# Six bases of layer two taken out of the TensorE contraction and added by VectorE, in a two-relation graph network on one core

## The chip, the cores and the metric

The kernel runs on one core of one Trainium2 chip. The metric is device time in microseconds of the whole launch, the median over several runs. A profiled execution gives a span (first to last instruction) beside its own time.

## The reference

Node features `x` are 625 x 512; 20,625 edges (10,000 drawn, their reverses, and self loops) have a type 0 or 1. The work is:

```
h   = gelu(batchnorm(GCN(x) with W, b)) + x
x1  = layernorm(x + h)
layer(v, basis, att, gate, root, bias):
    w[r] = sum_b att[r, b] * basis[b]                 # r = 0, 1;  b = 0..29;  basis[b] is 512 x 512
    msg  = sigmoid(v[col] . gate[r]) * v[col] @ w[r]  # r = the edge's type
    out  = segment_sum(msg, row) + v @ root + bias
x2  = layer(relu(layer(x1, basis1, ...)), basis2, ...)
out = layernorm(x1 + x2)
```

What matters here is the first line of `layer`: in each of the two layers two 512 x 512 weights are combined from thirty bases, 30 MB of f32 a layer, read from HBM.

## The kernel before

**The basis combination.** Each layer's weight is made in eight chunks `cc` (0 to 7 layer one, 8 to 15 layer two) of `SUB = 4` parts, 64 parts in all. A part is 1 MB: 8 bases by 16 rows on the 128 partitions, four rows (`JB`) of 512 in the free dimension. The last part of a chunk covers bases 22 to 29 with two of them masked to zero in `S`. SyncE loads part `n` into slot `n % 4` of `basis_ring` and for that waits until part `n - 4` is used (line 379). TensorE contracts a part in `basis_part` (line 495) into PSUM `psW`, one half for the even chunk, one for the odd. A pair of chunks gives one block `pp` of 128 rows of both weights: ScalarE's `w_first(pp)` masks the even half into `w_half`, VectorE's `w_merge(pp)` adds the odd half and shuffles it into `w_both` (lines 1007, 1009, 1011), ScalarE's `w_high(pp)` makes the rounded half (line 783) and VectorE's `w_low(pp)` the rest (line 1023) for three-matmul products in fp32r. `w_half` and `w_both` are single buffers. Blocks 0 to 3 are layer one, 4 to 7 layer two.

**The order around it.** All engines run fixed lists with semaphores. TensorE does basis parts in pairs between other products, by the lists given to `basis_upto`: behind the x1 transposes (L653), the root1 products (L476 to L478 with root tiles), the ten layer-one `Z` products (12 matmuls of 512 columns each), and the eight `h` products (L720, 20 matmuls each, four of 320 and four of 306 columns). `Z` results are turned into `zg` by ScalarE (L893) and then VectorE (L1216). Each `h` result is added to `r1T` by VectorE (L1242), relu'd by ScalarE (L908), and its low half made by VectorE (L1246). Then `gates_and_z(1)` starts layer two: gate rows, then Z, which needs all of blocks 4 to 7 (`w_lo`), and last the out products (L740). PSUM gives these products four banks in turn.

**GpSimd** makes the rstd powers (L452, L453), and issues the small root loads on its own queue: root1 (L435), and root2 (L460) once the last hlT is written, then bias2 (L464).

Of the kernel before, what the change touches and what calls it, by code (L numbers as in the profile page):

```python
# [38 lines left out]
P = 128  # L39
# [28 lines left out]
BG = P // KB  # L68
RING = 4
OH = 3 * G  # L70
KEYS = NC * WIN
# [7 lines left out]
def gnn_block(nc, x, src, dst, etype, W0, b0, gamma, beta,  # L79
# [28 lines left out]
    with ctx:  # L108
# [57 lines left out]
        mask_h = sb("mask_h", [P, 2], F32)  # L166
        S = sb("S", [P, 2, 2, SUB, KB, R], F32)
        vecT = sb("vecT", [P, KC, NV], F32)
        gw_hl = sb("gw_hl", [P, 2, KC, 2, R], F32R)
# [24 lines left out]
        basis_in = [sem(f"basis_in{i}") for i in range(RING)]  # L194
        basis_used = sem("basis_used")
        w_half, w_merged, w_both = sem("w_half"), sem("w_merged"), sem("w_both")
        w_hi, w_lo = sem("w_hi"), sem("w_lo")
# [127 lines left out]
        def bases(q):  # L325

            first = min(BG * q, NB - BG)
            return slice(first, first + BG)

        def own(q):  # L330

            return BG * q - bases(q).start
# [32 lines left out]
        def _(sp):  # L365
# [8 lines left out]
            def load(n):  # L374
                L, c, q = n // (CH * SUB), n // SUB % CH, n % SUB
# [3 lines left out]
                sp.dma_start(ring[:, n % RING].rearrange("p j o -> p (j o)"), rows[c // 2, c % 2]) \  # L379
                    .then_inc(basis_in[n % RING], 16)  # L380

            for n in range(2 * CH * SUB):
# [13 lines left out]
        def _(pool):  # L396
# [74 lines left out]
        def _(pe):  # L471
# [11 lines left out]
            def basis_part(n):  # L483

                cc, q = n // SUB, n % SUB
# [7 lines left out]
                pe.wait_ge(basis_in[n % RING], 16 * (n // RING + 1))  # L493
                for j in range(JB):
                    m = nc.tensor.matmul(psW[32 * j:32 * j + 32, cc % 2, :],  # L495
                                         S[:, cc % 2, cc // CH, q].rearrange("p k r -> p (k r)"),
                                         ring[:, n % RING, j, :], start=(q == 0), stop=(q == SUB - 1))
                m.then_inc(basis_used, 1)
# [174 lines left out]
            def gates_and_z(L):  # L673
# [72 lines left out]
        def _(act):  # L746
# [14 lines left out]
            def w_first(pp):  # L761

                act.wait_ge(basis_used, SUB * (2 * pp + 1))
                if pp:
# [5 lines left out]
            def w_high(pp):  # L770
# [7 lines left out]
                for r in range(R):  # L778
                    act.wait_ge(w_both, R * pp + r + 1)
                    hi, full = w_block(pp // KC, pp % KC)[:, r, 0, :], both[:, r, :]  # L780
# [84 lines left out]
            for h, (a, n) in enumerate(HALF):  # L865
                for f in range(KC):
# [6 lines left out]
                    if (h, f) == (1, 1):  # L873
                        w_high(4)
                        w_first(5)

            def gates_and_z(L):
                for h, (a, n) in enumerate(HALF):
# [3 lines left out]
                    act.sem_inc(free_act, 1)  # L882
                    act.sem_inc(gate_rows_ready, 1)
                wait_full(act, ("gate", L))
                ins = nc.scalar.activation(gate[:, L].rearrange("p c r -> p (c r)"), bank(("gate", L))[0:PC, 0:R * NC],
# [4 lines left out]
                for c in range(NC):  # L890
                    for r in range(R):
                        wait_full(act, ("Z", L, c, r))
                        nc.scalar.activation(zg[:, 0, c, r, :], bank(("Z", L, c, r))[0:PC, :], ACT.Copy,  # L893
                                             scale=gate[:, L, c, r:r + 1]).then_inc(zg_hi, 1)
                    if L == 0 and c == 2:
                        w_high(5)
                        w_first(6)
                    if L == 1 and c == 1:
# [4 lines left out]
            for h, (a, n) in enumerate(HALF):  # L903
                n = min(n, N - a)
                for f in range(KC):
                    i = KC * h + f
                    act.wait_ge(h_sum, i + 1)
                    nc.scalar.activation(hlT[:, 0, f, a:a + n], r1T[:, f, a:a + n], ACT.Relu).then_inc(t_hi, 1)  # L908
                    if i == 2:
                        w_high(6)  # L910
                        w_first(7)
            w_high(7)
            gates_and_z(1)


        @block.vector
        def _(dve):
# [83 lines left out]
            def w_merge(pp):  # L1001

                dve.wait_ge(w_half, R * (pp + 1))
                dve.wait_ge(basis_used, SUB * (2 * pp + 2))
                dve.wait_ge(w_hi, R * pp)
# [6 lines left out]
                dve.sem_inc(w_both, 1)  # L1012
                dve.sem_inc(w_merged, 1)

            def w_low(pp):
# [191 lines left out]
            w_merge(4)  # L1207
            w_low(4)

            def z_parts(L):  # L1210
                dve.wait_ge(gate_ready, L + 1)
                for c in range(NC):
                    for r in range(R):
# [6 lines left out]
                        dve.sem_inc(zg_ready, 1)  # L1220
                    if L == 0 and c == 1:
                        w_merge(5)
                    if L == 0 and c == 3:
                        w_low(5)
                    if L == 1 and c == 2:
# [8 lines left out]
            z_parts(0)  # L1234
            w_merge(6)
            for h, (a, n) in enumerate(HALF):
                n = min(n, N - a)
                for f in range(KC):
# [9 lines left out]
                        .then_inc(t_ready, 1)  # L1248
                    if i == 3:
                        w_low(6)  # L1250
                    if i == 6:
                        w_merge(7)
            w_low(7)
            z_parts(1)
            dve.wait_ge(bias2_in, 16)
            dve.wait_ge(basis_used, 2 * CH * SUB)
            for c in range(NC):
# [33 lines left out]
```

## Time and profile before

| | |
|---|---|
| median of 3 runs | 318.35 us (316.65 to 320.71) |
| profiled execution | 318.3 us, span 316.2 us |
| granted TensorE clock, mean | 0.957 |
| TensorE busy | 278.1 us (88%) |
| VectorE busy | 161.4 us (51%) |
| ScalarE busy | 87.4 us (28%) |
| GpSimd busy | 40.3 us (13%) |
| basis matmuls (L495) | 64.8 us busy, 512 records for 64 parts |
| HBM read | 72.05 MB |

Busy times of engines overlap, so they don't add up to the span. Two matmul records stand for one f32 basis matmul, eight for a part.

### The profile page before, as it was taken

The numbers are of one execution on the slowest core, as the hardware profiler recorded it, in microseconds if no ns is written. First come the engines' busy times: TensorE is split into PE (matmuls) and PEld (weight loads), VectorE is DVE, ScalarE is ACT, GpSimd is POOL, SyncE is SP. The second block draws the span as 40 slices with busy tenths as digits, with TensorE's granted clock in tenths as the row PEclk, the third lists the DMA queues.
The fourth block names the chain that finished last, engine by engine and source line by source line (L and its number), as shares of the span: only waits on it lengthen the run. The fifth ranks groups of instructions, "written<-read, shape, count | busy, mean of one in ns | idle before, by whom it ended". The sixth has DMA issues, their size and how long they took to land.

```text
span 316.2 us, 4593 instructions
## 1 busy us (share of the span) xinstructions
PE 278.1 (88%) x1687; PEld 184.8 (58%) x1687; DVE 161.4 (51%) x362; ACT 87.4 (28%) x137; POOL 40.3 (13%) x76
## 2 busy tenths in 40 slices
PE   1698958999699987659999999999997999999991
PEld 1583423343487554236766646677775777787770
DVE  3888888884575842983320141342425125334443
ACT  5250220201145848445152114111312242100000
POOL 2001000000294104510000000000004600010000
PEclk9999996999859997899999999999999999999997
DMA  6997992999938999986994977977101400001112
GB/s 174 241 417 295 338 403 82 410 379 401 367 86 274 343 421 419 423 313 262 335 399 158 421 287 288 425 282 262 77 0 43 126 0 0 0 2 32 32 32 65
DMA packets 12802, 73.63 MB, mean 233 GB/s; under 512 B 2000, under 2 KB 2243, under 8 KB 4588
## 3 DMA queue, kind: packets, MB, share of 16 engines
q1 hardware_dynamic: 11330, 70.82, 59.1%
q0 software_dynamic: 1104, 2.36, 2.7%
q8 instruction: 13, 0.21, 0.3%
q10 hardware_dynamic: 346, 0.17, 0.2%
q14 instruction: 9, 0.07, 0.1%
HBM read 72.05 MB, written 1.28 MB: 232 GB/s over the span
## 4 chain that ended last, share of the span: by engine, by line
PE 66%; DVE 12%; DMA 9%; issue 6%; DVEq 3%; SPq 1%; ACT 1%; POOL 1%; POOLq 0%; ACTq 0%
PE psW L495 15%; PE psM L476 9%; PE psM L478 8%; PE psM L477 8%; PE psM L720 7%; PE psM L740 6%; DMA basis_ring<-in_L_gnn_basis_dram 5%; DVE B L1037 3%; DMA w_raw<-in_L_gnn_W_dram 3%; PE psM L617 3%; PE psE L576 2%; PE psM L543 2%; DVEq L1027 2%; DVE oh_key L1044 1%; PE psM L599 1%
## 5 line engine op out<-in xcount | busy, mean ns | idle before, releaser
L495 PE MATMUL psW<-basis_ring,S 128*32 128x512 f32 x512 | 64.8, 624 | 5.4 <-DMA basis_ring<-in_L_gnn_basis_dram 3.3
L1216 DVE SCALAR_TENSOR_TENSOR zg<-psM,gate,zg 125x512 fp32r<-125x512 f32 x20 | 15.0, 750 | 56.9 <-ACT zg L893 56.9
L495 PEld LDWEIGHTS psW<-basis_ring,S 128*32 128x32 f32 x512 | 13.6, 112 | 38.8 <-issue 29.0
L476 PE MATMUL psM<-w,hlT 128*125 128x512 f32 x80 | 32.4, 406 | 0.1
L478 PE MATMUL psM<-w,hlT 128*125 128x512 f32 x80 | 31.7, 396 | 0.0
L477 PE MATMUL psM<-w,hlT 128*125 128x512 f32 x80 | 31.6, 395 | 0.0
L576 PEld LDWEIGHTS psE<-oh_key,oh_src 128*125 128x125 f16 x162 | 14.2, 146 | 22.4 <-issue 15.2
L893 ACT ACTIVATE zg<-psM,gate 125x512 fp32r<-125x512 f32 x20 | 13.8, 689 | 46.3 <-PE psM L478 45.9
L720 PEld LDWEIGHTS psM<-BB,zg 125*128 125x128 f32 x160 | 23.1, 188 | 3.4 <-issue 2.5
L720 PE MATMUL psM<-BB,zg 125*128 125x320 f32 (+1 forms) x160 | 24.1, 309 | 0.0
L740 PE MATMUL psM<-zg,BB 125*125 125x512 f32 x100 | 24.0, 394 | 0.0
L576 PE MATMUL psE<-oh_key,oh_src 128*125 128x160 f16 x162 | 17.4, 249 | 6.8 <-DVE B L1037 6.7
L1037 DVE TENSOR_TENSOR B<-B,psE 125x160 f32 x54 | 17.4, 323 | 11.0 <-issue 6.2
L543 PE MATMUL psM<-w0T,xT 128*125 128x512 f32 x40 | 21.7, 634 | 0.0
L460 POOL DMA_DIRECT2D root_raw<-in_L_gnn_root_dram x16 | 7.9, 503 | 105.4 <-DVE hlT L1246 105.4
L740 PEld LDWEIGHTS psM<-zg,BB 125*125 125x125 f32 x100 | 18.5, 185 | 4.7
L476 PEld LDWEIGHTS psM<-w,hlT 128*125 128x125 f32 x80 | 14.8, 185 | 9.0 <-issue 2.5
L617 PE MATMUL psM<-AT,z 125*128 125x320 f32 (+1 forms) x80 | 16.3, 354 | 3.1 <-DVE z L1117 3.1
L1044 DVE TENSOR_TENSOR oh_key<-iota_f,key_pairs 128x960 f16<-128x960 f16 x27 | 18.5, 685 | 0.3
L617 PEld LDWEIGHTS psM<-AT,z 125*128 125x128 f32 x80 | 13.3, 214 | 6.6 <-issue 5.7
L478 PEld LDWEIGHTS psM<-w,hlT 128*125 128x125 f32 x80 | 14.8, 185 | 3.8
L477 PEld LDWEIGHTS psM<-w,hlT 128*125 128x125 f32 x80 | 14.8, 185 | 3.4
(152 smaller groups left out, 383.2 us busy)
## 6 DMA issues: line engine op xcount, KB each, us to landing
basis_ring<-in_L_gnn_basis_dram SPq DMA_DIRECT2D x64, 1024.0 KB, 6.9
root_raw<-in_L_gnn_root_dram POOLq DMA_DIRECT2D x32, 64.0 KB, 2.1
xs<-in_x_dram SPq DMA_DIRECT2D x1, 1120.0 KB
out_dram<-xs SPq DMA_DIRECT2D x5, 224.0 KB
w_raw<-in_L_gnn_W_dram SPq DMA_DIRECT2D x4, 256.0 KB, 9.2
bias_b<-in_L_gnn_bias_dram POOLq DMA_DIRECT2D x1, 250.0 KB, 3.8
xs<-in_x_dram SPq DMA_DIRECT2D x1, 130.0 KB
out_dram<-xs SPq DMA_DIRECT2D x5, 26.0 KB
```

The costliest lines, as they stand in the source:

```text
L476: nc.tensor.matmul(o, l_hi, r_hi, start=start, stop=False)
L477: nc.tensor.matmul(o, l_hi, r_lo, start=False, stop=False)
L478: last[0] = nc.tensor.matmul(o, l_lo, r_hi, start=False, stop=stop)
L495: m = nc.tensor.matmul(psW[32 * j:32 * j + 32, cc % 2, :], S[:, cc % 2, cc // CH, q].rearrange("p k r -> p (k r)"), ring[:, n % RING, j, : ...
L543: last[0] = nc.tensor.matmul(bank(("xw", c))[0:PC, :], xT[:, k, n], w0T[:, k], start=(k == 0), stop=(k == KC - 1))
L576: nc.tensor.matmul(psE[0:PC, g % 2, at:at + KEYS], oh_src[:, g % 3, j * P:j * P + PC], oh_key[:, t % OH, :], start=(j % SG == 0), stop=(j ...
L617: last[0] = nc.tensor.matmul(bank(("agg0", f, h))[:, 0:n], z[:, i, s, f * P:(f + 1) * P], AT[:, s, a:a + n], start=(s == 0 and i == 0), st ...
L720: last[0] = nc.tensor.matmul(bank(("h", f, h))[:, 0:n], zg[:, i, d, r, f * P:(f + 1) * P], BB[:, at:at + n], start=(d + r + i == 0), stop= ...
L740: last[0] = nc.tensor.matmul(bank(("out", c))[0:PC, :], BB[:, at:at + PC], zg[:, i, d, r, :], start=False, stop=(d == NC - 1 and r + i == 2))
L1037: v.tensor_tensor(to, to, psE[0:PC, g % 2, h * KEYS:(h + 1) * KEYS] .rearrange("p (c t w) -> p c t w", c=NC, t=R), ALU.add).then_inc(win_a ...
L1044: return v.tensor_tensor(out, pair.unsqueeze(1).broadcast_to(shape), pairs[:, first:first + n].unsqueeze(2).broadcast_to(shape), ALU.is_equal)
L1216: link(v.scalar_tensor_tensor(out=zg[:, 1, c, r, :], in0=bank(("Z", L, c, r))[0:PC, :], scalar=gate[:, L, c, r:r + 1], in1=zg[:, 0, c, r, ...
```

## The change

In layer two a chunk has three parts (24 bases) instead of four; parts are 56 instead of 64. The first layer's ring keeps four slots, layer two's parts use slots 0 to 2. Slot 3 is used, once layer one's parts are done, for the last six bases: GpSimd's queue loads them in the weight's own row order, two bases by 128 rows of 512 to a piece (four DMAs, one for each 32 partitions), three pieces for a block, twelve in all, two at a time in the slot. VectorE adds each with `scalar_tensor_tensor` onto `w_both`, times the attention coefficient of that basis and relation (`rest_att`, a small broadcast load on SyncE's queue behind the fourth part): 12 adds a block, 48 in all. The orders of merges, high and low halves of layer two are laid anew.

```diff
+PARTS = [(cc, q) for cc in range(2 * CH) for q in range(SUB if cc < CH else SUB - 1)]
+LAST = [n for n, (cc, q) in enumerate(PARTS) if n + 1 == len(PARTS) or PARTS[n + 1][0] != cc]
+SLOT = [n % RING if cc < CH else (n - CH * SUB) % (RING - 1) for n, (cc, q) in enumerate(PARTS)]
+REST = NB - BG * (SUB - 1)
+PIECE = SUB // 2
+PIECES = REST // PIECE
...
+        def slot_before(n):
+            return max([i for i in range(n) if SLOT[i] == SLOT[n]], default=None)
...
-                if n >= RING:
-                    sp.wait_ge(basis_used, n - RING + 1)
+                if slot_before(n) is not None:
+                    sp.wait_ge(basis_used, slot_before(n) + 1)
...
+                    sp.dma_start(rest_att[:], att2[:, NB - REST:NB].unsqueeze(0).broadcast_to([P, R, REST])) \
+                        .then_inc(rest_att_in, 16)
...
+            pool.wait_ge(basis_used, CH * SUB)
+            for kc, i in itertools.product(range(KC), range(PIECES)):
+                m = PIECES * kc + i
+                if m >= 2:
+                    pool.wait_ge(w_added, R * PIECE * (m - 1))
+                b0 = NB - REST + PIECE * i
+                rows = basis2[b0:b0 + PIECE].rearrange("b (m c j) o -> c j m b o", m=2 * KB, c=KC)
+                for j in range(JB):
+                    pool.dma_start(ring[32 * j:32 * j + 32, RING - 1, PIECE * (m % 2):PIECE * (m % 2 + 1)], rows[kc, j]) \
+                        .then_inc(rest_in[m % 2], 16)
...
-                n = (n + 1) // 2 * 2 - 1
+                n = (n + 1) // 2 * 2 - 1 if n < CH * SUB else n
...
-                basis_upto((33, 35, 35)[c])
+                basis_upto((33, 34, 34)[c])
...
-                            basis_upto((45, 47, 47, 49, 51, 51, 53, 55, 55, 57)[R * c + r])
+                            basis_upto((45, 47, 47, 49, 51, 51, 53, 55, 55, 55)[R * c + r])
...
-                    basis_upto((57, 59, 59, 61, 61, 63, 63, 63)[KC * h + f])
...
+            def add_rest(kc, first, last):
+                for k in range(first, last):
+                    b, r = k // R, k % R
+                    m = PIECES * kc + b // PIECE
...
+                    if k % (R * PIECE) == 0:
+                        dve.wait_ge(rest_in[m % 2], 16 * JB * (m // 2 + 1))
+                    if k < R:
+                        dve.wait_ge(w_both, R * (KC + kc) + r + 1)
+                    else:
+                        dve.wait_ge(w_added, R * REST * kc + k - R + 1)
+                    v.scalar_tensor_tensor(out=both[:, r, :], in0=ring[:, RING - 1, PIECE * (m % 2) + b % PIECE, :],
+                                           scalar=rest_att[:, r, b:b + 1], in1=both[:, r, :],
+                                           op0=ALU.mult, op1=ALU.add).then_inc(w_added, 1)
```

The order in words. VectorE: block 4's merge is followed by its twelve adds, then `w_low(4)` and `w_merge(5)` ahead of layer one's zg operations; behind these go block 5's adds (four behind each of the first three), `w_low(5)` behind the fifth, `w_merge(6)` behind the sixth, and block 6's adds, three behind each of the last four. In the h stage `w_low(6)` and `w_merge(7)` follow step 1, block 7's adds stand three behind each of steps 2 to 5, and `w_low(7)` follows step 7. ScalarE: `w_high(4)` moves from the root1 products to behind the layer-one gate rows, `w_first(6)` behind the third zg, `w_high(5)` behind the fourth, `w_first(7)` behind the last, `w_high(6)` behind the h stage's first relu and `w_high(7)` behind its seventh. Layer two's high halves wait for `w_added` instead of `w_both`.

## Rows read from the trace of the kernel before

**Rows 1.** The page's slices: granted clock in 40 equal parts, tenths of full.
```profile
PEclk9999996999859997899999999999999999999997
```

**Rows 2.** Windows: stretch, length, busy PE, PEld, DVE, ACT, POOL, clock, DMA, GB/s.
```profile
119.00:127.00 8.00, 6.47 (x40) 3.66 (x44) 2.46 (x4) 6.38 (x8) 4.45 (x3) 0.79 1.01 421
...
150.00:165.00 15.00, 15.00 (x112) 10.52 (x105) 5.26 (x12) 5.10 (x10) 0.00 (x0) 1.00 0.96 362
165.00:207.00 42.00, 42.00 (x232) 25.66 (x229) 10.20 (x15) 10.28 (x17) 0.00 (x0) 1.00 0.81 322
```

**Rows 3.** Chain that ended last, 205 to 246: start, us, what.
```profile
207.23 1.85 PE psW L495 x16
...
230.77 1.85 PE psW L495 x16
232.62 3.04 PE psM L720 x20
...
235.69 0.48 DVE r1T L1242
...
242.66 0.49 PE psM L476
```

**Rows 4.** The same chain, 120 to 143.
```profile
132.75 3.21 PE psW L495 x16
...
141.73 0.73 DVE w_both L1011 x2
...
142.66 0.62 PE psW L495
```

**Rows 5.** Timeline of TensorE, two bursts with one Z product between.
```profile
169.67 1.92 PE L495 MATMUL psW<-basis_ring,S 128*32 128x512 f32 x16
...
174.51 1.92 PE L495 MATMUL psW<-basis_ring,S 128*32 128x512 f32 x16
```

**Rows 6.** Landing of basis loads (L379): 120 to 220, then 182 to 186.
```profile
DMA to landing us min/median/max: 4.7/6.3/8.8
...
DMA to landing us min/median/max: 4.7/5.5/6.4
```

**Rows 7.** GpSimd's loads: timeline of root2's issues; page, DMA issues.
```profile
241.56 7.89 POOL L460 DMA_DIRECT2D root_raw<-in_L_gnn_root_dram  x16 [105.39 <-DVE hlT L1246]
249.45 0.55 POOL L464 DMA_DIRECT2D bias_b<-in_L_gnn_bias_dram  x1
...
root_raw<-in_L_gnn_root_dram POOLq DMA_DIRECT2D x32, 64.0 KB, 2.1
...
bias_b<-in_L_gnn_bias_dram POOLq DMA_DIRECT2D x1, 250.0 KB, 3.8
```

**Rows 8.** Timeline of VectorE: a permuted low half, block 4's shuffle, the h stage.
```profile
138.12 2.01 DVE L1023 TENSOR_TENSOR w<-w_both,w 128x512 fp32r<-128x512 f32 x2 [0.25 <-DVE hlT L1191]
...
152.40 0.75 DVE L1011 STREAM_SHUFFLE w_both<-w_half 128x512 f32<-128x512 f32 x1
...
207.99 0.75 DVE L1216 SCALAR_TENSOR_TENSOR zg<-psM,gate,zg 125x512 fp32r<-125x512 f32 x1 [2.10 <-ACT zg L893]
...
212.26 0.49 DVE L1242 TENSOR_TENSOR r1T<-r1T,psM 128x320 f32<-128x320 f32 x1 [0.90 <-PE psM L720]
213.44 0.49 DVE L1246 SCALAR_TENSOR_TENSOR hlT<-r1T,hlT 128x320 fp32r<-128x320 f32 x1 [0.69 <-ACT hlT L908]
...
224.71 1.28 DVE L1023 TENSOR_TENSOR w<-w_both,w 128x512 fp32r<-128x512 f32 x2
...
241.31 1.29 DVE L1023 TENSOR_TENSOR w<-w_both,w 128x512 fp32r<-128x512 f32 x2
```

**Rows 9.** Timeline of ScalarE, gate rows to gate in layer one.
```profile
165.80 0.42 ACT L880 ACTIVATE gate_rows<-psM 4x306 f32<-4x306 f32 x1 [0.69 <-PE psM L683]
166.40 1.28 ACT L885 ACT_TABLE_LOAD   x1 [0.18 <-ACT gate_rows L880]
169.77 0.18 ACT L885 ACTIVATE gate<-psM 125x10 f32<-125x10 f32 x1 [2.09 <-PE psM L703]
```

More of the change, by code:

```diff
@@ L195, in gnn_block @@
         basis_used = sem("basis_used")
+        rest_att_in, rest_in, w_added = sem("rest_att_in"), [sem(f"rest_in{i}") for i in range(2)], sem("w_added")
         w_half, w_merged, w_both = sem("w_half"), sem("w_merged"), sem("w_both")
@@ L328, in bases, with parts_upto, slot_fills @@
             return slice(first, first + BG)
+        def parts_upto(cc):
+            return LAST[cc] + 1
+        def slot_before(n):
+            return max([i for i in range(n) if SLOT[i] == SLOT[n]], default=None)
+        def slot_fills(n):
+            return SLOT[:n + 1].count(SLOT[n])
         def own(q):
@@ L374, in load @@
             def load(n):
-                L, c, q = n // (CH * SUB), n // SUB % CH, n % SUB
-                if n >= RING:
-                    sp.wait_ge(basis_used, n - RING + 1)
+                cc, q = PARTS[n]
+                L, c = cc // CH, cc % CH
+                if slot_before(n) is not None:
+                    sp.wait_ge(basis_used, slot_before(n) + 1)
                 rows = (basis1, basis2)[L][bases(q)].rearrange("b (k h c j) o -> c h (b k) (j o)", k=KB, h=2, c=KC)
-                sp.dma_start(ring[:, n % RING].rearrange("p j o -> p (j o)"), rows[c // 2, c % 2]) \
-                    .then_inc(basis_in[n % RING], 16)
-            for n in range(2 * CH * SUB):
+                sp.dma_start(ring[:, SLOT[n]].rearrange("p j o -> p (j o)"), rows[c // 2, c % 2]) \
+                    .then_inc(basis_in[SLOT[n]], 16)
+            for n in range(len(PARTS)):
                 load(n)
@@ L483, in basis_part @@
             def basis_part(n):
-                cc, q = n // SUB, n % SUB
+                cc, q = PARTS[n]
                 if n == 0:
@@ L496, in basis_part @@
                                          S[:, cc % 2, cc // CH, q].rearrange("p k r -> p (k r)"),
-                                         ring[:, n % RING, j, :], start=(q == 0), stop=(q == SUB - 1))
+                                         ring[:, SLOT[n], j, :], start=(q == 0), stop=(n in LAST))
                 m.then_inc(basis_used, 1)
@@ L778, in w_high @@
                 for r in range(R):
-                    act.wait_ge(w_both, R * pp + r + 1)
+                    if pp < KC:
+                        act.wait_ge(w_both, R * pp + r + 1)
+                    else:
+                        act.wait_ge(w_added, R * REST * (pp - KC + 1) - (R - 1 - r))
                     hi, full = w_block(pp // KC, pp % KC)[:, r, 0, :], both[:, r, :]
@@ L883, in gates_and_z @@
                     act.sem_inc(gate_rows_ready, 1)
+                if L == 0:
+                    w_high(4)
                 wait_full(act, ("gate", L))
@@ L894, in gates_and_z @@
                                              scale=gate[:, L, c, r:r + 1]).then_inc(zg_hi, 1)
-                    if L == 0 and c == 2:
-                        w_high(5)
-                        w_first(6)
+                        if L == 0 and (c, r) == (1, 0):
+                            w_first(6)
+                        if L == 0 and (c, r) == (1, 1):
+                            w_high(5)
+                    if L == 0 and c == 4:
+                        w_first(7)
                     if L == 1 and c == 1:
@@ L908, in _ @@
                     nc.scalar.activation(hlT[:, 0, f, a:a + n], r1T[:, f, a:a + n], ACT.Relu).then_inc(t_hi, 1)
-                    if i == 2:
+                    if i == 0:
                         w_high(6)
-                        w_first(7)
-            w_high(7)
+                    if i == 6:
+                        w_high(7)
             gates_and_z(1)
@@ L1207, in _, with behind_z @@
             w_merge(4)
-            w_low(4)
+            add_rest(0, 0, R * REST)
+            def behind_z(step):
+                if step < 3:
+                    add_rest(1, 4 * step, 4 * step + 4)
+                if step == 4:
+                    w_low(5)
+                if step == 5:
+                    w_merge(6)
+                if step >= 6:
+                    add_rest(2, 3 * (step - 6), 3 * (step - 6) + 3)
             def z_parts(L):
+                if L == 0:
+                    w_low(4)
+                    w_merge(5)
                 dve.wait_ge(gate_ready, L + 1)
@@ L1220, in z_parts @@
                         dve.sem_inc(zg_ready, 1)
[L1221 to L1224, printed above, removed]
+                        if L == 0:
+                            behind_z(R * c + r)
                     if L == 1 and c == 2:
@@ L1234, in _ @@
             z_parts(0)
-            w_merge(6)
             for h, (a, n) in enumerate(HALF):
@@ L1248, in _ @@
                         .then_inc(t_ready, 1)
-                    if i == 3:
+                    if i == 1:
                         w_low(6)
-                    if i == 6:
                         w_merge(7)
+                    if 2 <= i < 6:
+                        add_rest(3, 3 * (i - 2), 3 * (i - 2) + 3)
             w_low(7)
@@ L1255, in _ @@
             dve.wait_ge(bias2_in, 16)
[L1256 removed]
+            dve.wait_ge(basis_used, len(PARTS))
             for c in range(NC):
```

11 lines of the change are left out of this document (7 added, 4 removed).

## The prediction

> **What bounds the kernel now.** I read the slices of the page first: TensorE is the engine that is busy nearly throughout, and its clock is near full but for a few slices, the lowest of them where it waited or had just waited [rows 1]. Nothing else is near full, except DMA: in three stretches its share is 1.01, 0.96 and 0.81, at 421, 362 and 322 GB/s [rows 2]. So a megabyte costs about 2.5 us of the DMA engines when they are saturated, and layer two's loads run close to that. Then the chain that ended last, around the change. In the h stage it is TensorE alone: bursts of two basis parts at 1.85 us (0.925 us a part) between the products, h products at 3.04 us for one of 20 matmuls; after TensorE's last h product ends at 235.66 the chain goes over VectorE and ScalarE, because the eighth merge, its high half and its low half all follow the last basis part, and the layer-two Z product starts at 242.66 [rows 3]. That is 7.0 us of handover. Ahead of it, at 142.66, another such place: TensorE waits for the fourth merge [rows 4].
>
> **What goes.** Eight of the 64 basis parts: 8 x 0.925 = 7.4 us of TensorE. Up to 207.23 the list of bursts keeps its places (two parts behind each), so all eight are the four bursts from 207.23 to 230.77 [rows 3]; they are on the path. 2 MB of 32 MB of layer-two traffic goes too. The small load of coefficients on SyncE's queue stands behind the fourth part and ahead of the fifth, which waits for the first part's use anyway; it is needed 130 us later: nothing. The merge of the last weight block no longer stands behind the last part in the h stage: its parts are done before the h products begin.
>
> **Part 35 moves behind a wait.** Three parts make a chunk, so part 35 opens the odd half and needs the fourth merge. Before, 34 and 35 ran ahead of it; now 35, 36 and 37 start together when the merge ends (before at 142.5). That costs 0.925 us. It gives a little back: 34 and 35 took 3.21 us ahead of the third x1 transpose, at a lowered clock [rows 4]; with one part gone that transpose is ready earlier, but ScalarE's and VectorE's order lets only about 0.25 us of it through to the merge. Net +0.7.
>
> **The ring of three.** Each burst of two frees its first slot 0.93 us before its end, and the second part of the next burst needs that slot's new load. Where one Z product stands between bursts, bursts start at 169.67 and 174.51, 4.84 us apart [rows 5], so a load has 4.8 us from release to need. The loads of this stretch land 4.7 us after issue at best, 6.3 in the median; the pair issued between 182 and 186 took 4.7 and 6.4 [rows 6]. Before, with four slots, such a load had a whole burst more. Six second parts are exposed (39, 41, 43, 47, 51, 55). Bound: nothing at 4.7 and no competitor, up to about 8 us if each is late by a half-megabyte piece (1.25 us at 421 GB/s). I take 1.5: 0.1 to 0.4 at each for the spread of first loads, plus a piece in the way at one of them, as most are issued while no piece is in flight.
>
> **GpSimd's pieces.** A piece is four DMAs of 64 rows of 2 KB. 32 rows take 7.89 / 16 = 0.49 us to issue and land in 2.1; bias2, read as 125 rows, takes 0.55 us and lands in 3.8 [rows 7]. The 64-row ones should lie between: 4 x 0.52 = 2.1 us of issue and 2.5 for the last to land, so 4.6 us from release to use; by the ends 4 x 0.49 + 2.1 = 4.1 and 4 x 0.55 + 3.8 = 6.0. GpSimd stands idle after its last rstd near 136; pieces 0 and 1 go then and are there before the fifth merge. Nothing that anybody needs stands behind them on that queue until root2, near 240.
>
> Its queue runs beside VectorE. In this trace the root2 issues begin at 241.56, inside the pair of two-input subtractions at 241.31 [rows 7, 8]: the pair takes 1.29 us, as the one at 224.71 takes 1.28, and the issues keep their mean of 0.49. The Trainium skill (SBUF — State Buffer, A bandwidth-pool intuition that's wrong) says that a VectorE operation in a two-port mode keeps GpSimd from writing its descriptors, and advises the hardware queues under VectorE work; its section Who interferes with whom adds that a tensor_tensor with two SBUF inputs takes only the read side. By the first the pieces would be late (third rival), by the second and by the row above they cost what I took.
>
> **VectorE's adds.** 48 scalar_tensor_tensor, 128x512, f32, both inputs in SBUF. Nearest row: the subtraction pair 128x512, two SBUF inputs, 1.28 us for two, so 0.64 to 0.66 each in a row and 0.75 for a last one [rows 8]. The other end is the same subtraction through permuted views, 2.01 us for two or 1.0 each [rows 8], which these adds don't use. An add waits only for the one two before it, which is long done. I take 0.66: 33 us in all, placed thus:
>
> Block 4: the fifth merge's shuffle starts at 152.40 [rows 8]; with the shift VectorE is free at 153.9. Eight adds take until 159.2; piece 2 is released after four (156.6) and lands at 161.3; the last four end at 164.2. ScalarE now takes the high half after the gate rows, which it finished at 166.2, and the gate's sigmoid ran at 169.77 [rows 9]: 1.7 us of slack, then 1.14 us of copying and the 1.28 us table load still fit ahead of 169.8 + 0.7. Hidden. If that cover goes, gate, zg and in time TensorE wait behind it, since both engines run in order.
>
> Blocks 5 and 6: four adds (2.7 us) behind each of three zg operations of 0.75, where steps come every 2.8 or 4.8 us; one zg is late by about 1 us, and three further PSUM banks cover it. Then three adds (2.05) behind each of the last four. Hidden, except that the last three stand behind the last zg, where TensorE no longer pauses for a burst.
>
> Block 7 is where cover ends. **The h stage becomes VectorE's.** A step of it holds VectorE 1.67 us, from the r1T addition at 212.26 to the end of the hlT one at 213.93, the ScalarE relu between them included [rows 8]; TensorE makes one each 3.0 us. Counted from TensorE's end of the last Z product (207.2 before): last zg done +1.7; gap and three adds +4.0; steps 0 and 1 +7.4; w_low(6) 1.3 and w_merge(7) 2.2 with gaps +11.2; four times a step and three adds (1.65 + 2.05) +26.0; piece 11, released only after four of these adds and needed some 4.2 us later, +0.4; steps 6 and 7 +29.7; w_low(7) 1.3, +31.0. TensorE alone would need 24.0 for the h products, so it waits some 4 us before the last gate rows and the Z product.
>
> **Sum.** Z of layer two starts at 207.2 + 0.7 + 1.5 + 31.0 = 240.4, against 242.66: 2.3 us earlier. Of the 7.4 us, 2.2 go to part 35 and the ring, 7 to VectorE's chain behind the h products, and 4 come back from the shorter handover. Behind that point order and waits are as before (root2 still starts with the last hlT, 1.3 us ahead of Z). The profiled execution took 318.3 us around its span of 316.2, the median is 318.35: 318.3 - 2.3 = **316.0 us**.
>
> **Rivals.**
> (1) TensorE stays the bound of the h stage. If the steps' waits on ScalarE overlap with adds or the adds run faster, VectorE keeps up, and the handover is a step and w_low(7), 3.1 us: 207.2 + 0.7 + (0 to 1.5) + 24.0 + 3.1 = 235.0 to 236.5, so 310.6 to 312.1. For it: VectorE's busy time is low. Against it: its order is fixed and the steps' 0.7 us waits stay inside.
> (2) The ring of three starves TensorE: the slower side. Place: second parts of bursts one product apart, 4.8 us after release. It decides at a landing of about 5.6 us: above 0.8 us at each of the exposed six the wait reaches 4.8, more than my 1.5 plus the 2.3 gain. With each load 2.5 us later (a megabyte of competing traffic, since the pieces share 16 DMA engines that were 0.96 busy [rows 2]) it would be 6 x 2.5 = 15, less 1.5: 329.5; half of that, 322 to 325. For it: 6.3 us median. Against it: most of those medians are second loads of a pair.
> (3) Pieces come late because VectorE holds GpSimd up: each issue stretched by one add, 0.5 to 1.16 us, a piece by 2.6. Blocks 4 and 6 had 1.7 and 0.8 us of slack, piece 11 none: about +0.9, +1.8 and +2.6, of which some 4 reach the end: 320. This is the Trainium skill's rule named above. The row at 241.56 speaks against it, though only few issues overlap there.
> (4) The adds cost 1.0 instead of 0.66: 15 adds on the path x 0.34 = +5.1, 321.
>
> **How the numbers follow.** Forecast 0.52 (312.5 to 318.5), rival 1 0.16, rival 2 0.18, rival 3 0.07, rival 4 0.07. A measurement of this kernel tells about 2% from no change: 312.0 and 324.7 are the bounds. Faster is rival 1 with little ring waiting and a small tail of the forecast, 0.17; slower is over half of rival 2, with little of the others, 0.12; the rest, 0.71, within. The range goes from rival 1's lower part to rival 4: 311 to 321.5, which leaves out the heavier half of rival 2 and a little below.
>
> **What the new profile would show.** 448 basis matmuls instead of 512; no basis part after Z; adds of L-basis tiles at 0.66 to 0.75 us, three behind each h step; TensorE idle before the last gate rows with VectorE's hlT as releaser; Z of layer two near 240. Rival 2 shows as idle time of TensorE on basis loads between 150 and 207; rival 3 as GpSimd issues above 0.6 us and adds waiting for DMA. I would be wrong first if the waits on ring loads sum to more than 3 us, or if VectorE's chain from Z to Z is far from 31 us.

## The result and the profile after

The changed kernel takes 331.92 us (329.51 to 336.31 over 5 runs) against 318.35: the ratio is 1.042, with a 95% interval of 1.037 to 1.047. The forecast was 316.0 and the range ended at 321.5. Here and below medians and spreads are over all runs, while a ratio and its interval compare only those runs of a kernel that lie within 1.5% of its fastest. The execution that was profiled is one of the longer ones, with a span of 334.3 us; a second profile of the same kernel, with a span of 324.5, stands beside it in the table below, and nothing here rests on a difference that only one of the two shows.

The page of the kernel after: clock and DMA slices, the costliest groups, and the DMA issues with KB and median us to landing.

```profile
PEclk9999987999579999699989995999995999999995
DMA  6998984999569999979999999524022400001112
GB/s 176 247 392 274 375 358 149 375 405 393 202 166 387 373 425 350 286 296 367 276 301 260 306 313 319 222 64 128 0 63 52 106 0 2 0 0 33 32 32 61
...
L529 PE MATMUL psW<-basis_ring,S 128*32 128x512 f32 x448 | 59.3, 632 | 16.1 <-DMA basis_ring<-in_L_gnn_basis_dram 15.4
L1068 DVE SCALAR_TENSOR_TENSOR w_both<-basis_ring,rest_att,w_both 128x512 f32<-128x512 f32 x48 | 33.0, 747 | 17.4 <-DMA basis_ring<-in_L_gnn_basis_dram 15.4
L489 POOL DMA_DIRECT2D basis_ring<-in_L_gnn_basis_dram x48 | 25.5, 538 | 84.0 <-DVE w_both L1068 84.0
...
basis_ring<-in_L_gnn_basis_dram SPq DMA_DIRECT2D x56, 1024.0 KB, 8.3
basis_ring<-in_L_gnn_basis_dram POOLq DMA_DIRECT2D x48, 128.0 KB, 5.2
```

The 448 matmuls, the 33.0 us of adds and the 0.54 us of an issue are as costed. What is not: TensorE waits 15.4 us for ring loads (3.3 before), VectorE 15.4 us for pieces, and a ring load lands after 8.3 us in the median (6.9 before). In slices 21 to 25 (167 to 209 us) the DMA engines are at 9 tenths or more throughout, yet move only 260 to 319 GB/s; before, the stretch from 150 to 165 gave 362 at a share of 0.96 [rows 2]. The windows of the kernel after say it in numbers (length, busy time of the five engines, clock, DMA share, GB/s):

```profile
155.00:205.00 50.00, 39.17 (x224) 22.33 (x223) 24.79 (x41) 12.51 (x21) 12.70 (x24) 0.93 1.00 299
...
248.00:256.40 8.40, 3.30 (x18) 1.66 (x16) 5.54 (x11) 2.73 (x6) 1.72 (x4) 0.76 0.05 10
256.40:276.00 19.60, 19.60 (x84) 15.55 (x84) 3.76 (x5) 5.84 (x8) 6.68 (x14) 0.93 0.25 63
```

TensorE's timeline of the kernel after shows where the waits fall: behind the first part of a burst, at the second, which has to wait for its slot to be filled again. Before, no part of this stretch waited: the bursts are whole, at 1.92 us [rows 5].

```profile
155.44 1.06 PE L529 MATMUL psW<-basis_ring,S 128*32 128x512 f32 x8
157.74 1.07 PE L529 MATMUL psW<-basis_ring,S 128*32 128x512 f32 x8 [1.23 <-DMA basis_ring<-in_L_gnn_basis_dram]
...
162.32 1.06 PE L529 MATMUL psW<-basis_ring,S 128*32 128x512 f32 x8
...
166.59 1.63 PE L529 MATMUL psW<-basis_ring,S 128*32 128x512 f32 x8 [3.20 <-DMA basis_ring<-in_L_gnn_basis_dram]
...
185.07 1.06 PE L529 MATMUL psW<-basis_ring,S 128*32 128x512 f32 x8 [1.88 <-DMA basis_ring<-in_L_gnn_basis_dram]
...
202.52 1.94 PE L529 MATMUL psW<-basis_ring,S 128*32 128x512 f32 x8 [2.05 <-DMA basis_ring<-in_L_gnn_basis_dram]
```

Next, the landing of the four ring loads issued between 156 and 172 by SyncE, and of the eight DMAs of pieces 2 and 3, issued by GpSimd between 156 and 164 (kernel after). A ring load took 4.7 at best and 8.8 at most from 120 to 220 before [rows 6]; here four took 10.0 to 12.7.

```profile
DMA to landing us min/median/max: 10.0/12.5/12.7
...
DMA to landing us min/median/max: 5.9/9.5/15.4
```

VectorE's timeline of the kernel after: eight adds of block 4 go at 0.66 us each, then it stands for 11.38 us before the last four.

```profile
154.03 5.39 DVE L1068 SCALAR_TENSOR_TENSOR w_both<-basis_ring,rest_att,w_both 128x512 f32<-128x512 f32 x8 [0.35 <-DVEq L1052]
170.80 2.74 DVE L1068 SCALAR_TENSOR_TENSOR w_both<-basis_ring,rest_att,w_both 128x512 f32<-128x512 f32 x4 [11.38 <-DMA basis_ring<-in_L_gnn_basis_dram]
...
254.30 1.28 DVE L1080 TENSOR_TENSOR w<-w_both,w 128x512 fp32r<-128x512 f32 x2
```

The chain of the kernel after ends the h stage as forecast, over VectorE's steps and adds; layer two's Z starts at 256.64 (256.44 by the timeline), 31.7 us after the first h product at 224.96. Between the first two lines shown it also passes over the last piece, number 11: its issue and landing take 4.3 us, but VectorE stands only 0.42 us for it, as the forecast had it.

```profile
238.09 2.07 DVE w_both L1068 x3
...
249.31 1.99 DVE w_both L1068 x3
...
254.44 2.20 PE psM L717 x8
256.64 0.43 PE psM L510
```

The first six of its matmuls stand 0.43 us apart where the same ones stood 0.23 apart before: TensorE idled for 5 of the 8.4 us ahead, and the granted clock of that window is 0.76, of the next 0.93 (1.0 before). Last, SyncE's waits of the kernel after. The closing barrier (L114) took 0.2 us before:

```profile
SPq L114 <- PEq L114: 3.4, 1, 3.4
```

Four marks on TensorE's timeline divide each profiled execution: first Z product of layer one, first h product, first Z product of layer two, end of the span (us). Each line is one execution:

| kernel | Z, layer one | h | Z, layer two | end | Z to h | h to Z | Z to end |
|---|---|---|---|---|---|---|---|
| before | 165.6 | 209.0 | 242.7 | 316.2 | 43.4 | 33.7 | 73.5 |
| changed | 173.2 | 225.0 | 256.4 | 334.3 | 51.8 | 31.4 | 77.9 |
| changed, second profile | 167.0 | 215.8 | 247.1 | 324.5 | 48.8 | 31.3 | 77.4 |
| ring of three, 64 parts | 165.4 | 209.2 | 242.8 | 316.4 | 43.8 | 33.6 | 73.6 |
| no pieces | 169.0 | 211.9 | 242.8 | 317.6 | 42.9 | 30.9 | 74.8 |
| no pieces, no adds | 169.7 | 212.4 | 238.5 | 312.0 | 42.7 | 26.1 | 73.5 |
| one wide DMA a piece | 167.3 | 212.3 | 243.1 | 317.8 | 45.0 | 30.8 | 74.7 |
| every fourth partition | 171.7 | 214.9 | 246.1 | 323.3 | 43.2 | 31.2 | 77.2 |
| pieces by SyncE | 169.7 | 226.2 | 257.2 | 332.2 | 56.5 | 31.0 | 75.0 |

Against before both profiles of the changed kernel lose 5.4 to 8.4 us between Z and h, where a burst less (1.85) should have made it shorter, and about 4 behind the second Z; they win 2.3 in the h stage. The place of the first mark varies by itself: in the kernels with a shorter handover and with 48 small DMAs, whose order up to there is that of before, it stands at 167.9 and 163.7.

### The profile page after: what moved, and what is told of

The parts are those of the page before. It is cut to its first block, busy times and chain, and to the rows that moved or that the text cites. A ratio compares the mean times of both kernels' runs of the same rounds, so it can differ in the third digit from the quotient of the medians.

```text
span 334.3 us, 4567 instructions
## 1 busy us (share of the span) xinstructions
PE 277.6 (83%) x1623; PEld 186.6 (56%) x1623; DVE 193.4 (58%) x410; ACT 87.8 (26%) x137; POOL 65.7 (20%) x124
## 4 chain that ended last, share of the span: by engine, by line
PE 51%; DMA 20%; DVE 17%; issue 6%; DVEq 1%; ACT 1%; POOL 1%; ACTq 0%; POOLq 0%
DMA basis_ring<-in_L_gnn_basis_dram 18%; PE psW L529 10%; PE psM L510 7%; PE psM L511 7%; PE psM L512 7%; PE psM L773 6%; PE psM L577 3%; PE psM L651 3%; PE psE L610 2%; PE psM L754 2%; DVE B L1094 2%; DVE w_both L1068 2%; DVE x_sum L1226 1%; PE psM L717 1%; DMA rows_i<-in_edge_type_dram 1%
## 5 line engine op out<-in xcount | busy, mean ns | idle before, releaser
L529 PE MATMUL psW<-basis_ring,S 128*32 128x512 f32 x448 | 59.3, 632 | 16.1 <-DMA basis_ring<-in_L_gnn_basis_dram 15.4
L1068 DVE SCALAR_TENSOR_TENSOR w_both<-basis_ring,rest_att,w_both 128x512 f32<-128x512 f32 x48 | 33.0, 747 | 17.4 <-DMA basis_ring<-in_L_gnn_basis_dram 15.4
L489 POOL DMA_DIRECT2D basis_ring<-in_L_gnn_basis_dram x48 | 25.5, 538 | 84.0 <-DVE w_both L1068 84.0
L529 PEld LDWEIGHTS psW<-basis_ring,S 128*32 128x32 f32 x448 | 10.9, 112 | 48.9 <-issue 25.9
L510 PE MATMUL psM<-w,hlT 128*125 128x512 f32 x80 | 33.6, 420 | 0.0
L511 PE MATMUL psM<-w,hlT 128*125 128x512 f32 x80 | 32.7, 409 | 0.0
L512 PE MATMUL psM<-w,hlT 128*125 128x512 f32 x80 | 32.6, 407 | 0.0
L610 PEld LDWEIGHTS psE<-oh_key,oh_src 128*125 128x125 f16 x162 | 14.3, 146 | 22.5 <-issue 17.3
L754 PE MATMUL psM<-BB,zg 125*128 125x320 f32 (+1 forms) x160 | 23.2, 306 | 0.0
L510 PEld LDWEIGHTS psM<-w,hlT 128*125 128x125 f32 x80 | 15.6, 195 | 9.7 <-issue 4.2
L1101 DVE TENSOR_TENSOR oh_key<-iota_f,key_pairs 128x960 f16<-128x960 f16 x27 | 17.7, 654 | 0.3
L512 PEld LDWEIGHTS psM<-w,hlT 128*125 128x125 f32 x80 | 15.5, 194 | 4.1
L511 PEld LDWEIGHTS psM<-w,hlT 128*125 128x125 f32 x80 | 15.6, 195 | 3.6
```

The lines of the kernel that those rows point to most:

```text
L489: pool.dma_start(ring[32 * j:32 * j + 32, RING - 1, PIECE * (m % 2):PIECE * (m % 2 + 1)], rows[kc, j]) \
L510: nc.tensor.matmul(o, l_hi, r_hi, start=start, stop=False)
L511: nc.tensor.matmul(o, l_hi, r_lo, start=False, stop=False)
L512: last[0] = nc.tensor.matmul(o, l_lo, r_hi, start=False, stop=stop)
L529: m = nc.tensor.matmul(psW[32 * j:32 * j + 32, cc % 2, :], S[:, cc % 2, cc // CH, q].rearrange("p k r -> p (k r)"), ring[:, SLOT[n], j, :] ...
L610: nc.tensor.matmul(psE[0:PC, g % 2, at:at + KEYS], oh_src[:, g % 3, j * P:j * P + PC], oh_key[:, t % OH, :], start=(j % SG == 0), stop=(j ...
```

## Experiments

Eleven kernels and the changed one again. Two theories are told apart first: D (depth: three slots are too few) and T (traffic: the pieces slow the ring loads). All times below are medians; ratios are to the kernel before on the same chip. Medians of two changed kernels are sometimes from different chips; the medians of before on them lie between 317.7 and 318.4 us.

### Without the pieces

```diff
-            pool.wait_ge(basis_used, CH * SUB)
-            for kc, i in itertools.product(range(KC), range(PIECES)):
-                ...                                      # the 48 DMAs
-                    if k % (R * PIECE) == 0:
-                        dve.wait_ge(rest_in[m % 2], 16 * JB * (m // 2 + 1))
```

> The changed kernel with the twelve piece loads left out (48 DMAs on GpSimd's queue); VectorE adds what lies in slot 3, so the last six bases are not added. The changed kernel takes 331.9 us against 318.35. Theory T (traffic): ring loads land late because the pieces are in flight beside them; without pieces the waits of TensorE on ring loads fall from 14 us to under 3, VectorE's chain from Z to Z stays near 31 us, and the time is 314 to 318. Theory D (depth): three slots are too few by themselves; the waits stay above 8 us and the time is above 324.

317.58 us (316.73 to 320.31, 10 runs), ratio 0.998 [0.994, 1.001]. All 14.3 us go with the loads of the pieces. The window 165 to 205 of this kernel, and TensorE's waits from 119 to 260:

```profile
165.00:205.00 40.00, 39.24 (x222) 23.55 (x226) 22.34 (x34) 11.87 (x19) 0.00 (x0) 1.00 0.77 290
```

```profile
PEld psW L519 <- DMA basis_ring<-in_L_gnn_basis_dram: 9.2, 7, 2.3
...
PE psW L519 <- DMA basis_ring<-in_L_gnn_basis_dram: 4.7, 5, 1.4
```

TensorE still waits 4.7 us for ring loads in this stretch, none over 1.4 us; I had expected under 3. It waited 2.2 us before.

### Ring of three alone

```diff
+SLOT = [n % RING if n < CH * SUB else (n - CH * SUB) % (RING - 1) for n in range(2 * CH * SUB)]
-                    sp.wait_ge(basis_used, n - RING + 1)
+                    sp.wait_ge(basis_used, max(i for i in range(n) if SLOT[i] == SLOT[n]) + 1)
```

(the kernel before, with SLOT[n] for n % RING wherever the ring is indexed)

> The kernel before, all 64 parts and no adds, but layer two's parts use slots 0 to 2 only. Theory D: 324 us or more. Theory T: a load has 4.8 us and lands in 4.7 or a little more, so waits sum to 1 to 3 us: 319 to 321.

319.44 us (318.40 to 321.19, 10 runs), ratio 1.0048 [1.0013, 1.0084]: 1.5 us for the missing slot, with all 64 parts. Theory D falls as the main cause. TensorE's waits for ring loads from 119 to 260 are, before, with this ring of three, and in the kernel after:

```profile
PE psW L495 <- DMA basis_ring<-in_L_gnn_basis_dram: 2.2, 2, 1.4
...
PE psW L496 <- DMA basis_ring<-in_L_gnn_basis_dram: 4.6, 5, 1.4
...
PE psW L529 <- DMA basis_ring<-in_L_gnn_basis_dram: 14.1, 10, 3.2
```

So the kernel without pieces, at 4.7 us, waits about as long as the ring of three does by itself. What the missing slot costs beside the pieces' traffic was not tried; the two may make each other worse.

### What about the pieces: queue, number, source rows or destination

```diff
# one wide DMA a piece (rows permuted)
-                rows = basis2[b0:b0 + PIECE].rearrange("b (m c j) o -> c j m b o", m=2 * KB, c=KC)
-                for j in range(JB):
-                    pool.dma_start(ring[32 * j:32 * j + 32, RING - 1, ...], rows[kc, j])
+                rows = basis2[b0:b0 + PIECE].rearrange("b (p c) o -> c p b o", c=KC)
+                pool.dma_start(ring[:, RING - 1, ...], rows[kc])
# neighbouring source rows
+                rows = basis2[b0:b0 + PIECE].rearrange("b (c j m) o -> c j m b o", m=2 * KB, c=KC)
# every fourth partition
+                    pool.dma_start(ring[j:P:JB, RING - 1, ...], rows[kc, j])
```

> The changed kernel with each piece fetched by one DMA over 128 partitions instead of four over 32: same bytes, same 2 KB rows, same queue, another order of rows, so that the last six bases are added permuted. If it is the four narrow destinations that slow the DMA engines (theory T-narrow), loads beside pieces land in under 8 us and the time falls to about 319 to 323. If any traffic from the second queue does it (T-queue), the time stays at 329 to 333.

324.16 us (318.81 to 329.00, 10 runs), a wide scatter, which stays unexplained: only the second shortest execution (319.70) has a profile. The ratio is 1.009 [1.003, 1.014]. By the median it is 7.5 us less than the 331.66 of the changed kernel below, though a little above the 319 to 323 expected. So T-queue, that any traffic from the second queue does it, falls.

> The changed kernel with each of the four DMAs of a piece reading 32 neighbouring rows of a basis instead of rows 16 apart; destination and sizes are the same, the rows of the last six bases are added in another order. If the distance of the source rows slows the loads (T-source) the time falls by 5 us or more; by T-narrow and T-queue it stays at 329 to 333.

335.35 us (329.85 to 337.87, 4 runs): no gain from nearer source rows, and even a little above the 329 to 333 expected. T-source falls.

> The changed kernel with the four DMAs of a piece writing to every fourth partition (j, j+4, ...) instead of 32 neighbouring ones; 48 DMAs, bytes and source rows as in the changed kernel, the last six bases added with permuted rows. T-narrow (a destination of 32 neighbouring partitions holds up all DMA engines): the time falls to 320 to 325, like the one wide DMA. T-count (four DMAs on the queue instead of one, whatever their destination): stays at 329 to 334.

325.04 us (322.51 to 329.91, 4 runs), ratio 1.017 [1.008, 1.027]. Nothing differs from the changed kernel but the partitions that a DMA writes; the number of DMAs, their bytes and their source rows are the same. T-count falls, T-narrow stands.

> The changed kernel unedited, on the same chip as the three others, as their reference: 330 to 333 us, with TensorE's waits on ring loads between 10 and 16 us and ring loads beside pieces landing after 8 us or more.

331.66 us (326.55 to 334.36, 4 runs), ratio 1.045 [1.037, 1.054], whose interval lies above that of the strided one. The medians differ by 6.6 us; with four runs each, whose spreads overlap, that size is rough. The profile is of its shortest run (TensorE waits 9.0 us for ring loads in it, below the 10 to 16 expected) and is only 1.2 us longer than the strided one's, so it is the rate of the DMA engines that is to be compared. Windows 165 to 205, first of the changed kernel (second profile), then of the strided one:

```profile
165.00:205.00 40.00, 34.85 (x190) 20.07 (x187) 23.91 (x40) 11.19 (x18) 8.43 (x16) 0.96 1.01 324
```

```profile
165.00:205.00 40.00, 38.76 (x213) 22.91 (x214) 24.57 (x41) 11.06 (x18) 8.82 (x16) 0.96 0.89 342
```

With neighbouring partitions the DMA engines are full at 324 GB/s; with every fourth one they move 342 at 0.89. TensorE is busy 3.9 us more in that stretch, but the strided kernel had come to its first Z 4.7 us later, and the two reach the h stage 0.9 us apart. The rate divided by the share doesn't depend on such shifts. From 155 to 205 us, in eight profiles:

| kernel | pieces written to | DMA share | GB/s | GB/s divided by share |
|---|---|---|---|---|
| changed | 32 neighbours | 1.00 | 299 | 299 |
| changed, second profile | 32 neighbours | 1.01 | 324 | 321 |
| neighbouring source rows | 32 neighbours | 0.94 | 298 | 317 |
| pieces by SyncE | 32 neighbours | 1.02 | 322 | 316 |
| every fourth partition | every fourth | 0.91 | 348 | 382 |
| every fourth, by SyncE | every fourth | 0.92 | 352 | 383 |
| one wide DMA a piece | all 128 | 0.91 | 347 | 381 |
| no pieces | none | 0.80 | 302 | 378 |

For a full share the four with narrow pieces move 299 to 321 GB/s, the four others 378 to 383. That holds for short and long executions alike, and is the firmest evidence here. Alone the narrow form is nearly harmless. Landing of GpSimd's pieces in the h stage, where no ring load runs, in the changed kernel (220 to 232) and in the strided one (205 to 228):

```profile
DMA to landing us min/median/max: 2.7/2.8/3.8
```

```profile
DMA to landing us min/median/max: 2.3/2.4/4.2
```

So the price arises where narrow writes and ring loads share the 16 DMA engines. The Trainium skill (SBUF — State Buffer, Door 1: The DMA port swizzle) says that bits 2 to 4 and 6 of the partition number pick the port: by it 32 neighbouring partitions reach 8 of 16 ports, every fourth one reaches all. The two kernels differ in just the partitions that a DMA writes, and the runs agree; that it is the ports and not something else that goes with these partitions is the word of the Trainium skill, no run here shows a port.

### Another queue

```diff
+            rest_after = {35: (0, 1), 43: (2,), 44: (3,), 46: (4,), 48: (5,), 49: (6,), 51: (7,), 55: (8, 9, 10, 11)}
             for n in range(len(PARTS)):
                 load(n)
+                for m in rest_after.get(n, ()):
+                    rest(m)                              # the piece's four DMAs, on SyncE's queue
```

> The changed kernel with the twelve pieces issued by SyncE, on the queue of the ring loads, at fixed places between them (behind the loads of parts 35, 43, 44, 46, 48, 49, 51, 55); destinations as in the changed kernel. If two queues in turn on the same DMA engines are what stretches the ring loads, a load then waits only for whole pieces ahead of it (1.3 us each) and the time falls to 319 to 324. If the narrow destination is slow by itself, it stays above 326.

333.45 us (331.94 to 336.20, 4 runs), ratio 1.049 [1.039, 1.058]. Two queues in turn are not what costs: on one queue the narrow pieces cost as much.

> Pieces on SyncE's queue as in the run before (333.5 us with 32 neighbouring partitions), but each DMA writes to every fourth partition; the last six bases are added with permuted rows. If the narrow destination is the main price whatever the queue, the time falls by 6 us or more, to 320 to 327. If on this queue it is the order of the loads that costs, it stays above 330.

324.91 us (322.96 to 327.80, 4 runs), ratio 1.024 [1.018, 1.031]: 8.5 us less than with neighbouring partitions. By the medians the narrow destination costs 6.6 us on the one queue and 8.5 on the other.

### Without the adds

```diff
             def add_rest(kc, first, last):
-                for k in range(first, last):
-                    ...
+                pass
```

(and layer two's high halves wait for `w_both`, as before)

> The changed kernel without the piece loads and without the 48 adds on VectorE: the last six bases of layer two are left out. With loads out but adds in it took 317.6 us and its h stage was VectorE's chain (31 us from Z to Z). If that chain is what eats the eight parts saved, as the prediction had it, Z to Z falls to 27 to 28 us and the time to 311 to 313. If the adds were covered elsewhere and something else holds the h stage, the time stays at 316 to 318.

313.14 us (311.94 to 314.33, 4 runs), ratio 0.983 [0.976, 0.991]. Taking the adds away from the kernel without pieces is worth 4.4 us. In the table it is 4.8 us in the h stage (30.9 with adds, 26.1 without; I had expected 27 to 28) and 1.3 behind the second Z, less 0.5 ahead of the h stage. This is what the eight parts saved bring when nothing is put in their place: 5 of 7.4 us.

### The closing barrier

The kernel before with small DMAs on GpSimd's queue that nobody reads:

```diff
+            for i in range(48):                          # or 24
+                j = i % 4
+                if i >= 4:
+                    pool.wait_ge(spare_in[j], 16 * (i // 4))
+                pool.dma_start(spare[32 * j:32 * j + 32, :], x[32 * j:32 * j + 32, 0:64]).then_inc(spare_in[j], 16)
```

> The kernel before with 48 small DMAs added to GpSimd's queue (32 rows of 256 bytes of x into a spare buffer, nobody reads it), issued while GpSimd is idle ahead of root2. Theory C: that many DMAs on GpSimd's queue lengthen the closing barrier, on which SyncE waited 3.4 us in the changed kernel and 0.2 before; then this one has the 3.4 us too and takes 321 to 322. Otherwise the closing wait stays at 0.2 and the time at 318 to 319.

321.27 us (319.42 to 323.91, 10 runs), ratio 1.010 [1.006, 1.014].

> The same with 24 small DMAs, 57 in all on that queue against 81 and 33. If the closing wait grows with their number it is about 1.6 us and the time 319.5 to 320; if it steps at some number, it is 0.2 or 3.4.

318.61 us (316.31 to 321.33, 10 runs), ratio 1.0005 [0.996, 1.005]. SyncE's wait at the closing barrier with 48, then with 24 small DMAs:

```profile
SPq L108 <- PEq L108: 3.3, 1, 3.3
```

```profile
SPq L108 <- PEq L108: 1.4, 1, 1.4
```

With 33, 45, 57 and 81 DMAs on GpSimd's queue (before, one wide DMA a piece, 24 small, 48 small or changed) the wait is 0.2, 0.4, 1.4 and 3.3 to 3.4 us. With the pieces on SyncE's queue (33 on GpSimd's) it is 0.2 again. From 57 to 81 that is 0.08 us a DMA; by that slope, as an estimate, the first 40 or so cost nothing. With 24 the wait grew by 1.2 us, but the time stayed within the noise of 318, below the 319.5 to 320 expected. The trace names TensorE's queue as the last to arrive; that the time is GpSimd's own at its end is inferred from its number of DMAs, not seen.

### A shorter handover

The table of before and the kernel without adds both suggest that the handover behind the h products is a cost of order, not of work. The kernel before with its own 64 parts and ring of four:

```diff
-                    basis_upto((57, 59, 59, 61, 61, 63, 63, 63)[KC * h + f])
+                    basis_upto((59, 61, 63, 63, 63, 63, 63, 63)[KC * h + f])
# ScalarE: w_high(6) behind step 0, w_first(7) behind 1, w_high(7) behind 4 (before: 2, 2, 7)
# VectorE: w_low(6) behind step 1, w_merge(7) behind 3, w_low(7) behind 5 (before: 3, 6, 7)
```

> The kernel before with all 64 parts and a ring of four, only that the last six parts follow h steps 0, 1 and 2 instead of 1, 3 and 5, and the eighth merge, its high half and its low half follow steps 3, 4 and 5. The handover behind the h products (7.0 us before) should fall to about 3.5, with VectorE's last hlT and the gate rows in it; as the seventh step's merge also hid some of it, the gain is 1 to 2 us: 316.5 to 317.5. If the handover is not what it seems (loads late, merges in the way), the time stays at 318.

317.04 us (314.32 to 319.07, 12 runs) against 318.37: ratio 0.995 [0.992, 0.998]. Small, but its interval lies below 1, and it beats both kernels. Its chain from the last burst to the second layer's Z:

```profile
224.54 1.85 PE psW L495 x16
226.39 14.43 PE psM L720 x100
...
240.85 0.48 DVE r1T L1244
...
241.51 0.47 ACT hlT L908
...
242.00 0.49 DVE hlT L1248
...
242.53 1.29 PE psM L683 x8
243.82 0.23 PE psM L476
```

From the end of TensorE's last h product to Z it is 3.0 us (240.82 to 243.82), of which 1.3 are gate rows. The prediction put the same stretch of the kernel before at 7.0 us, from 235.66 to 242.66 [rows 3]. That is a misreading: at 235.66 the chain leaves TensorE behind the seventh h product. TensorE's timeline of before shows products seven and eight in one row of 40 matmuls, which ends with the gate rows' start at 238.3:

```profile
232.55 5.92 PE L720 MATMUL psM<-BB,zg 125*128 125x306 f32 x40
238.31 1.34 PE L683 MATMUL psM<-hlT,gw_hl 128*4 128x320 f32 x8
241.33 1.29 PE L683 MATMUL psM<-hlT,gw_hl 128*4 128x306 f32 x8 [1.67 <-DVE hlT L1246]
```

So the handover was 4.3 us and fell to 3.0; that is the 1.4 us by which h to Z shrinks in the table (33.7 to 32.3), and the 1.3 us of the medians.

## Why the prediction was wrong

The step that failed is the price of the pieces' traffic, in two terms of the sum: how late a ring load comes beside pieces, and when a piece lands. It is worth about 11 of the 15.9 us between forecast and measurement; a closing barrier that the sum didn't have is another 3.2. Without the piece loads the kernel takes 317.6 us, 1.6 above the forecast. By its own steps:

**What bounds the kernel now**: the 7.0 us of handover were 4.3, as shown above. The forecast's time doesn't use the 7.0: it starts from 207.2 and compares with 242.66, so this error changed its account of the 7.4 us but not the number.

**What goes**: right. 448 matmuls; without adds and pieces 313.1 us, 5.0 of the 7.4 us.

**Part 35 behind a wait**: its size can't be read from one mark. The three parts start at 141.64 in the changed kernel, against 142.66 [rows 4], but the burst behind the fourth merge starts anywhere from 140.8 (ring of three) to 143.4 (shorter handover) in kernels with the order of before. From that burst's start to the first Z product it is 22.9 us before, 24.6 with the ring of three and 27.2 without pieces. Of the last one's 4.3 us more than before, 0.9 is the part itself, 2.0 are waits on ring loads (1.4 with the ring of three alone), and 0.8 is that its three parts took 3.56 us at a granted clock of 0.77, where they take 2.78 at 1.00 in the changed kernel's second profile; 0.6 is left. The forecast had 0.7 for the part.

**The ring of three**: 1.5 us was right for the ring by itself (1.5 measured), though TensorE's waits for ring loads grew by 2.4 us. Beside the pieces it failed. It allowed 8 us at most, by counting a piece in the way as its bytes at 421 GB/s, 1.25 us. Beside narrow pieces four loads took 10.0 to 12.7 us instead of 4.7 to 8.8, single waits reached 3.2 us, and the whole transfer slowed for as long as the two were mixed: for a full share 299 and 321 GB/s in the two profiles, against 378 without pieces.

**GpSimd's pieces**: the issue was right (0.54 for 0.52), the landing wrong. 2.5 us was read from root2 and bias2, which run when nothing else does; the pieces land in 2.8 us in such a place too, but in 5.9 to 15.4 beside ring loads. The row that would have warned was there: a DMA share of 0.96 from 150 to 165 [rows 2] leaves little room for another queue. So VectorE stood 11.4 us ahead of block 4's last adds, where I had counted 1.7 us of slack.

**VectorE's adds**: right: 0.67 us each in a row of eight, 33.0 us in sum, so the fourth rival's 1.0 us did not come. That GpSimd would be held up by them (third rival) did not happen either: the four issues at 157.06 take 2.12 us inside the adds from 154.03 to 159.42, and eight take 4.30 us at 135.34, ahead of the first add.

**The h stage becomes VectorE's**: right. 31.0 us forecast from the last Z product of layer one to the first of layer two, 31.4 and 31.3 measured from the first h product; the adds there cost 4.8 us. Some of the match is luck: VectorE's last low half ended 30.6 us after the first h product, and Z came 0.9 later because the gate rows ran at the lowered clock (2.20 us, 1.29 before).

**Behind Z** the sum had nothing, with the words that order and waits are as before. It is 4 us: 3.2 of closing barrier, which the small DMAs give an unchanged kernel too, and about 1 of TensorE's clock, at 0.93 behind the handover instead of 1.0. Without pieces, where the barrier is short, 1.3 us remain with the same lowered clock.

The second rival had the right place, late ring loads at second parts, and as price 322 to 329.5, still below the 331.9 measured; it had a chance of 0.18. What it lacked was a reason for loads to be late by more than a piece's bytes, and the second victim, VectorE. The 14.3 us that the pieces cost divide by the medians into 6.6 for the narrow destination (331.7 to 325.0), 3.2 for the closing barrier, and 4.5 left over for six megabytes of traffic in a wide form beside a ring of three. That last term is only a difference: the two kernels with wide or strided pieces and a short barrier stand 6.6 (one wide DMA) and 7.3 us (strided, by SyncE) above the one without pieces. No run takes the traffic's price apart further.

## What to carry to other kernels

Price a new transfer in the stretch where it will run, not where a like one runs alone: 128 KB to 32 neighbouring partitions landed in 2.8 us alone and in up to 15 beside megabyte loads, and slowed those too. If a load must be cut by partitions and runs beside other loads, cut it so that each DMA touches partitions all over the array. Work moved from the bounding engine to an idle one is free only up to the next handover; here 4.4 of the 7.4 us came back by the medians as a chain of in-order VectorE work at the end of a stage, and moving the last merges earlier alone gave 0.5% with nothing removed. And a chain that ended last may leave an engine before its last work is done: read the end of an engine's work from its own timeline.

## What the runs showed of the hardware

- The destination of a small DMA decides what it costs others: every fourth partition instead of 32 neighbours, all else equal, is 6.6 us (GpSimd's queue) and 8.5 us (SyncE's) in 332, by medians of four runs each. For a full share of the DMA engines they moved 299 to 321 GB/s beside narrow pieces, 378 to 383 beside strided, wide or no pieces.
- The closing barrier waits 0.2, 0.4, 1.4 and 3.3 us with 33, 45, 57 and 81 DMAs on GpSimd's queue.
- TensorE restarted at 1.2 GHz after it had been idle for 5 of 8.4 us (clock 0.76 in that window, the next six matmuls 0.43 us apart instead of 0.23); after 6.6 us in which it was busy for 4.9 the clock stayed at 1.00 and they came 0.23 us apart.
